# Two attention blocks on one core: query and key rows copied by transfers, masks as extra rows, neighbour products on GpSimd, attention values in one full-precision product

## What is computed

```python
# block 1 (_L1_conv_ref): attention over all 1024 positions
q = bn(q_w @ x); k = bn(k_w @ x)               # 16 rows each
v = bn(v_w @ x)                                # 128 rows
attn = softmax(einsum('bci,bcj->bij', q, k), axis=-1)
x = gamma * einsum('bcj,bij->bci', v, attn) + x
# block 2 (_L2_conv_ref)
af, sf = relu(bn(wa @ x)), relu(bn(ws @ x))    # 16 rows each
att = softmax(where(adj, af^T sf, NEG), axis=2)    # adj: the 8 neighbours of a pixel
h_s = einsum('bnm,bcm->bcn', att, x)
Gc = einsum('bcn,bdn->bcd', x, x)
catt = softmax(where(|c - d| == 1, Gc, NEG), axis=2)   # the two neighbour channels
x = (1 - gama) * x + gama * elu(h_s + catt @ x)
```

## Time and profile before

| | us |
|---|---|
| median of 3 runs | 290.1 (289.94 to 290.49) |
| the profiled execution | 290.33 |
| its span in the trace | 288.5 |
| PE busy | 272.3 |
| DVE busy | 213.2 |
| ACT busy | 186.2 |
| POOL busy | 95.1 |

### The profile page before, as it was taken

How to read it: one execution, slowest core, us unless ns; L and a number is a source line. 1 busy time by engine, 2 the same in 40 slices (tenths; PEclk the granted TensorE clock), 3 DMA queues, 4 the chain that set the end, 5 groups by cost and what they waited for, 6 DMA issues and landing times.

```text
span 288.5 us, 4440 instructions
## 1 busy us (share of the span) xinstructions
PE 272.3 (94%) x1499; PEld 178.6 (62%) x1499; DVE 213.2 (74%) x325; ACT 186.2 (65%) x355; POOL 95.1 (33%) x102
## 2 busy tenths in 40 slices
PE   7999999999999899999999999799999799999994
PEld 3846555467677576747657464467867557765462
DVE  3865889789998786763489867799788775828383
ACT  0774676789997474766648776688748457674320
POOL 1045031505236878128004101354279814000000
PEclk9999999999999999999999999979999999999998
DMA  6951000000000000000000000000000000000015
GB/s 184 353 202 51 0 1 1 2 0 1 3 0 1 0 2 0 1 3 0 0 3 1 0 2 1 1 0 2 1 0 2 1 0 3 2 4 0 2 73 220
DMA packets 4520, 8.14 MB, mean 28 GB/s; under 512 B 1118, under 2 KB 2014, under 8 KB 4498
## 3 DMA queue, kind: packets, MB, share of 16 engines
q1 hardware_dynamic: 4498, 7.85, 7.8%
HBM read 5.68 MB, written 2.10 MB: 27 GB/s over the span
## 4 chain that ended last, share of the span: by engine, by line
PE 66%; DVE 10%; POOL 8%; ACT 8%; issue 3%; DMA 2%; SPq 1%; DVEq 0%; POOLq 0%; ACTq 0%
PE psum L360 64%; POOL e1h L1047 4%; ACT e L686 3%; DVE e1l L900 3%; DMA qs<-row 2%; ACT psum L677 2%; POOL ks L1040 1%; DVE nmax L884 1%; POOL qs L1037 1%; SPq L348 1%; DVE nmax L850 1%; ACT qs L669 1%; POOL regionb L1010 1%; ACT ks L670 1%; DVE x L860 1%
## 5 line engine op out<-in xcount | busy, mean ns | idle before, releaser
L1047 POOL CAST e1h<-e 128x1024 fp32r<-128x1024 f32 x32 | 42.6, 1333 | 34.7 <-ACT e L686 21.6
L900 DVE TENSOR_TENSOR e1l<-e,e1h 128x1024 fp32r<-128x1024 f32 x32 | 40.8, 1282 | 9.8 <-POOL e1h L1047 9.7
L686 ACT ACTIVATE e<-psum 128x1024 f32<-128x1024 f32 x32 | 32.8, 1025 | 20.6 <-DVE e1l L900 15.7
L850 DVE TENSOR_REDUCE nmax<-psum 128x1 f32<-128x1024 f32 x32 | 39.0, 1221 | 9.3 <-PE psum L360 8.7
L657 ACT ACTIVATE e<-psum,nmax 128x1024 f32<-128x1024 f32 x32 | 35.7, 1115 | 14.2 <-issue 9.6
L884 DVE TENSOR_REDUCE nmax<-psum 128x1 f32<-128x1024 f32 x32 | 38.0, 1217 | 3.9 <-PE psum L360 3.8
L677 ACT ACTIVATE psum<-psum,nmax 128x1024 f32<-128x1024 f32 x32 | 34.8, 1089 | 7.0 <-DVE nmax L884 6.3
L360 PE MATMUL psum<-e,v0n 128*64 128x512 f32 x128 | 31.0, 604 | 0.0
L360 PE MATMUL psum<-ks,qs 96*128 96x512 f32 (+2 forms) x96 | 30.1, 405 | 0.8 <-DVE ks L874 0.4
L360 PE MATMUL psum<-qs,ks 96*128 96x512 f32 (+2 forms) x96 | 28.9, 389 | 1.8 <-DMA qs<-row 1.3
L360 PE MATMUL psum<-xh 128*128 128x512 f32 x64 | 28.3, 442 | 0.6 <-DVE x L860 0.3
(11 more groups left out here) (175 smaller groups left out, 491.4 us busy)
## 6 DMA issues: line engine op xcount, KB each, us to landing
out<-xin SPq DMA_DIRECT2D x8, 256.0 KB, 2.1
xin<-in_x SPq DMA_DIRECT2D x3, 512.0 KB, 6.1
twist<-in_twist_in SPq DMA_DIRECT2D x1, 768.0 KB, 7.4
zz<-in_region_in SPq DMA_DIRECT2D x2, 360.0 KB, 3.5
xin<-in_x SPq DMA_DIRECT2D x2, 256.0 KB, 2.8
untwist<-in_untwist_in SPq DMA_DIRECT2D x1, 512.0 KB, 7.2
zz<-in_near_in SPq DMA_DIRECT2D x1, 288.0 KB, 4.4
rw<-in_rows_w SPq DMA_DIRECT2D x1, 256.0 KB, 2.7
```

What stands on the lines that cost most here:

```text
L686: inc(go(e1[:, E1_AT[b, i], :], t[:, :], ACT.Exp), "e1_ready", b)
L850: inc(vec.tensor_reduce(nmax0[z][:, i:i + 1], t[:, :], AX.X, ALU.max, negate=True), "nmax0_ready", b)
L900: inc(vec.tensor_tensor(e1l[:, EH_AT[b, i], :], e1[:, E1_AT[b, i], :], e1h[:, EH_AT[b, i], :].bitcast(F32), ALU.subtract), "e1l_ready", b)
L1047: done(gp.tensor_copy(e1h[:, EH_AT[b, i], :], e1[:, E1_AT[b, i], :]), "e1h_ready", b, i)
```

## The change

- **q, k, a, s rows.** The projection repeats the 64 rows for both halves on 128 partitions. ACT writes the rounded 128x512 tile `hi` in one instruction, DVE the low part `lo` in one. SP copies them into `qs` and `ks` (now three groups of 17 rows, R = 17): eight transfers of 17 rows of 2048 bytes from `hi` (`qkhi`, `ashi`), four from `lo` (`qklo`, `aslo`). `score` and `near` wait for all twelve (`qk_in`, 192 counts). GpSimd's copies are gone, the bias of q and k is added by ACT and DVE.
- **Mask rows.** Once for each of the four tiles `qs` and `ks` (two each), SP copies 29 further rows of 4352 bytes (`nearin`), whose product with each other is hugely negative outside the neighbourhood. A near window is then one product; the mask product is gone.
- **Channel products.** Only the products of neighbour channels are formed: GpSimd multiplies `x2T` by itself shifted by a channel (`cprod`, 128x1016) and adds in three steps (`csum`, 508, 254 and 127 elements); PE has three float32 products of two, one and one columns. DVE spreads the two weights back to a matrix (three small instructions).
- **Values.** `attL`, `e1h`, `e1l` and the split of the values are gone: `attH` is one full float32 product for each half, two for each tile.
- Rings: `RING0` 5 to 7, `STAGE` 2 to 5. All order tables are new; SP has one of its own.

```diff
-RING0 = 5
-STAGE = 2
-RING = 3
+RING0 = 7
+STAGE = 5
+SP_STEPS = steps(
+    "qklo.0.0 regin.0.0 nearin.0.0 qkhi.0.0 row1.0.0 qkhi.1.0 qklo.1.0 row1.1.0 ashi.0.0 aslo.0.0 row2.0.0 "
...
+            def rows(dst, at, src, k, z):
+                for h in range(2):
+                    o = h * 2 * G + k * G
+                    sp.dma_start(dst[z][at * R:(at + 1) * R, W + h * HALF:W + (h + 1) * HALF].bitcast(F32),
+                                 src[z][o:o + R, :].bitcast(F32)).then_inc(s["qk_in"][z], 16)
...
+                elif name == "nearin":
+                    wait(sp, "nearr_ready", 0)
+                    for k in range(2):
+                        for n, dst in enumerate((qs, ks)):
+                            sp.dma_start(dst[k][KS3:KS4, :].bitcast(F32),
+                                         nearr[n * 32:n * 32 + MASKS, :].bitcast(F32)).then_inc(near_sem, 16)
...
+                elif name in ("qkhi", "ashi"):
+                    wait(sp, "hi_ready", b, int(name == "ashi"))
+                    for dst, at, k in ((qs, 0, 0), (ks, 0, 1), (qs, 1, 0), (ks, 2, 1)):
+                        rows(dst, at, hi, k, z)
+                elif name in ("qklo", "aslo"):
+                    wait(sp, "low_ready", b, int(name == "aslo"))
+                    for dst, at, k in ((qs, 2, 0), (ks, 1, 1)):
+                        rows(dst, at, lo, k, z)
...
                 elif name == "score":
-                    wait(pe, "dup_ready", b, 3)
-                    wait(pe, "low_ready", b, 1)
+                    pe.wait_ge(s["qk_in"][z], ROWS_IN * (b // 2 * 2 + 1))
...
                 elif name == "attH":
-                    wait(pe, "e1h_ready", b, i)
+                    wait(pe, "e1_ready", b, i)
...
-                    for k, vv in enumerate((v1h[z], v1l[z])):
-                        for h in range(2):
-                            ho = slice(h * HALF, (h + 1) * HALF)
-                            mm(t[:, ho], vv[:, i, :], e1h[:, EH_AT[b, i], ho], i == 0 and k == 0, False)
...
+                        last = mm(t[:, ho], v1[z][:, i, :], e1[:, E1_AT[b, i], ho], i == 0, i == CH - 1)
...
                 elif name == "chan":
-                    for u in range(CH):
-                        mm(t[:, 0:P], x2T[z][:, u, :], x2T[z][:, u, :], u == 0, False)
-                    end(step, mm(t[:, 0:P], identb[:], chainb[:], False, True))
+                    mm(t[:, 0:2], ident, edge[:], True, False, True)
+                    mm(t[:, 0:1], cgram[:, 0:P], one[:], False, False, True)
+                    end(step, mm(t[:, 1:2], cgram[:, 1:P + 1], one[:], False, True, True))
...
-                        mm(t[:, w0:w0 + WIN], identb[:], nearb[:, kind, :], first, False, True)
-                        last = mm(t[:, off:off + hi - lo], lhs[:, u * P:(u + 1) * P], rhs[:, lo:hi],
-                                  False, not first, True)
+                        last = mm(t[:, w0:w0 + WIN], lhs[:, W + u * P:W + (u + 1) * P], rhs[:, u * P:u * P + WIN],
+                                  True, True)
...
-                    inc(go(qs[z][0:G, hc], t[q, 0:HALF], func), "qhi_ready", b)
-                    inc(go(ks[z][2 * G:3 * G, hc], t[k, 0:HALF], func), "khi_ready", b)
+                        inc(go(hi[z][:], t[:, 0:HALF], ACT.Identity, bias=bias[:, QK:QK + 1]), "hi_ready", b)
```

More of the change, by code:

```diff
@@ L22 @@
 G = 32
-KS3 = 3 * G
+R = HID + 1
+KS3 = 3 * R
+MASKS = 29
+KS4 = KS3 + MASKS
 WIN = P + 2 * W
 WPAD = 256
+NW = N + 2 * W
+NEG = -2.0 ** 53
 M = 16
@@ L150 @@
     gram=lambda i: [("e0_ready", i)], mix=lambda i: [("x1_ready", 1)],
-    qkproj=lambda i: [("low_ready", 1)], asproj=lambda i: [("low_ready", 3)], val1=lambda i: [("v1_ready", 0)],
+    qkproj=lambda i: [("low_ready", 0)], asproj=lambda i: [("low_ready", 1)], val1=lambda i: [("v1_ready", 0)],
     score=lambda i: [("sum1_ready", i)], shift1=lambda i: [("row_ready", 0)], shift2=lambda i: [("row_ready", 1)],
@@ L216, in conv_seq @@
         xrow = sb("xrow", [P, 2 * P])
-        ident = sb("ident", [P, P])
-        chain = sb("chain", [P, P])
+        beside = sb("beside", [P, P + 2])
+        ident, above, below = beside[:, 1:P + 1], beside[:, 0:P], beside[:, 2:P + 2]
+        edge = sb("edge", [P, 2])
+        one = sb("one", [P, 1])
         turn = sb("turn", [P, 2 * P])
@@ L380, in _ @@
                     pe.wait_ge(s["wfold_ready"][0], 3)
-                    pe.wait_ge(s["ones_ready"][0], 1)
+                    pe.wait_ge(fill_ready, 1)
                     t = begin(step)
                     for k in range(3):
-                        last = nc.tensor.transpose(t[:, k * P:(k + 1) * P], rws[:, k, :], ident[:])
-                    for k in range(2):
-                        last = nc.tensor.transpose(t[0:3, (3 + k) * P:(4 + k) * P], bias3[:, k, :], ident[:])
-                    end(step, last)
+                        last = nc.tensor.transpose(t[:, k * P:(k + 1) * P], rws[:, k, :], ident)
+                    end(step, nc.tensor.transpose(t[0:3, 3 * P:4 * P], bias3[:], ident))
                 elif name == "gap":
@@ L596, in _ @@
                     t = begin(step)
-                    end(step, nc.tensor.transpose(t[:, 0:P], coef[z], ident[:]))
+                    end(step, nc.tensor.transpose(t[:, 0:P], coef[z], ident))
                 elif name == "i1":
@@ L663, in _ @@
                 elif name in ("qkproj", "asproj"):
-                    first, func = (0, ACT.Copy) if name == "qkproj" else (2, ACT.Relu)
-                    t = take((name, b, 0))
-                    if first:
-                        wait(act, "e1_ready", b, CH - 1)
-                    q, k = slice(2 * i * G, (2 * i + 1) * G), slice((2 * i + 1) * G, (2 * i + 2) * G)
-                    inc(go(qs[z][0:G, hc], t[q, 0:HALF], func), "qhi_ready", b)
-                    inc(go(ks[z][2 * G:3 * G, hc], t[k, 0:HALF], func), "khi_ready", b)
+                    t = take(step)
+                    if name == "qkproj":
+                        inc(go(hi[z][:], t[:, 0:HALF], ACT.Identity, bias=bias[:, QK:QK + 1]), "hi_ready", b)
+                    else:
+                        inc(go(hi[z][:], t[:, 0:HALF], ACT.Relu), "hi_ready", b)
                 elif name == "val1":
                     t = take(step)
-                    inc(go(v1h[z][:].rearrange("p u c -> p (u c)"), t[:, :], ACT.Copy), "v1h_ready", b)
+                    inc(go(v1[z][:].rearrange("p u c -> p (u c)"), t[:, :], ACT.Copy), "v1_ready", b)
                 elif name == "score":
@@ L862, in _ @@
                 elif name in ("qklow", "aslow"):
-                    first = 0 if name == "qklow" else 2
-                    t = take((name[:2] + "proj", b, 0))
-                    for hi, rows, ready, dst, to in ((qs[z], 2 * i, "qhi_ready", qs[z], 2), (ks[z], 2 * i + 1, "khi_ready", ks[z], 1)):
-                        exact = t[rows * G:(rows + 1) * G, 0:HALF]
-                        at = slice(0, G) if to == 2 else slice(2 * G, 3 * G)
-                        low = dst[to * G:(to + 1) * G, hc]
-                        wait(dve, ready, b, first + i)
-                        if first:
-                            last = vec.scalar_tensor_tensor(out=low, in0=exact, scalar=0.0, in1=hi[at, hc].bitcast(F32),
-                                                            op0=ALU.max, op1=ALU.subtract)
-                        else:
-                            last = vec.tensor_tensor(low, exact, hi[at, hc].bitcast(F32), ALU.subtract)
-                    inc(last, "low_ready", b)
-                elif name == "val1":
-                    t = take(step)
-                    wait(dve, "v1h_ready", b)
-                    inc(vec.tensor_tensor(v1l[z][:].rearrange("p u c -> p (u c)"), t[:, :],
-                                          v1h[z][:].rearrange("p u c -> p (u c)").bitcast(F32), ALU.subtract),
-                        "v1_ready", b)
+                    n = int(name == "aslow")
+                    t = take((name[0:2] + "proj", b, 0))
+                    wait(dve, "hi_ready", b, n)
+                    by, op = (0.0, ALU.max) if n else (bias[:, QK:QK + 1], ALU.add)
+                    inc(vec.scalar_tensor_tensor(out=lo[z][:], in0=t[:, 0:HALF], scalar=by, in1=hi[z][:].bitcast(F32),
+                                                 op0=op, op1=ALU.subtract), "low_ready", b)
                 elif name == "score":
@@ L1009, in _ @@
                     settle()
[L1010 removed]
+                    done(gp.tensor_copy(regionb[:, i], region), "regions_ready", 0, i)
                     if i == 1:
@@ L1133, in _pack @@
         rows_p[:, V, n] = i["L1_conv_v_" + part]
-    for g in range(2):
-        at = slice(g * G, g * G + HID)
+    for h, g in ((0, 0), (0, 1), (1, 0), (1, 1)):
+        at = slice((2 * h + g) * G, (2 * h + g) * G + HID)
         pre = "L1_conv_k_" if g else "L1_conv_q_"
```

250 lines of the change are left out of this document (132 added, 118 removed), and 150 rows, old and new, of tables (ACT_STEPS, DVE_STEPS, PE_TEXT, POOL_STEPS).

## The result

| | before | after |
|---|---|---|
| median of the runs, us | 290.3 (289.9 to 290.8, 4 runs) | 457.0 (455.2 to 458.3, 4 runs) |
| ratio to before, 95% interval | | 1.574 [1.568, 1.580] |
| span of the profiled execution | 288.5 | 453.5 |
| PE busy / idle | 272.3 / 16.2 | 301.4 / 152.1 |
| PE busy at half clock, as recorded | 3.4 | 61.6 |

The account below looks back on a forecast made before the run. PE's work plus its waits was taken to bound the kernel (PE busy 272.3 of 288.5 us). Work and vanishing waits -5.8, transfer waits +140.7 and clock +13.6 on 290.3 gave 438.8, said as 438; range 302 to 475 for 8 in 10.

Parts of the forecast that it names:

- One engine for 17 and 29 rows, about 24 GB/s: Row and mask transfers: a prime row count runs on one DMA engine, 1.45 us per 17-row transfer, 5.26 per mask transfer.
- The waits: PE between projection and score: first wait 37.0 us, seven others 103.7 in sum, +140.7 us in all.
- Covers: PE's work between a projection and its score, which hides part of the transfers: 4.0 to 7.6 us for the seven.
- Waits that go, -2.9: PE's waits of 1.5 and 1.4 us for GpSimd's copies vanish; bounds 0 and -9 for lighter engines giving PE more.
- The clock, +13.6: Half clock behind eight long PE waits, 1.7 us lost each; bounds 0 and 27.
- PE's work, -2.9: PE's own work: values +10.4, near windows -7.0, channel product -5, bias products -1.3 us.
- near windows: Mask and score product of 0.22 us become one of 0.11, 64 times: -7.0 us, bounds nothing and 8.5 gained.
- channel product: PE's mask and eight products of 1.92 us become three small ones of 0.7, four times: -5 us.
- values: 64 full float32 products of 0.86 us replace 192 one-pass matmuls of 0.2325 on PE: +10.4 us.
- bias products: Four pairs of bias products leave PE: -1.3 us, between -0.9 and -1.9.
- Channel products on GpSimd, latency: GpSimd's product and sums on the way to `chan`: bounds 0 to 18 us, taken at 0.
- The sum: Profiled execution 290.3 - 5.8 + 140.7 + 13.6 = 438.8 us; 438 was said.

Follow-up runs that it names:

- e1: Changed kernel with 18 rows for 17 in each q and k row transfer, 29-row mask transfers kept; 378.3 us, ratio 1.302.
- e2: Changed kernel with 19 rows for 17 in each row transfer; 470.4 us, ratio 1.619.
- e3: Changed kernel with 32 rows in each row transfer and 32 mask rows for 29, the added rows zeros; 337.2 us, ratio 1.161.
- e11: Kernel before with mask rows, full-precision values and channel products on GpSimd, all but the row transfers; 299.1 us, ratio 1.030.
- e12: Kernel before with mask rows and full-precision values, without channel products on GpSimd; 288.8 us, ratio 0.995.
- e5: Kernel before with the channel products on GpSimd alone, their steps moved as in the change; 304.9 us, ratio 1.050.
- e7: Kernel before with mask rows and channel products on GpSimd, engine copies and split values kept; 299.9 us, ratio 1.035.
- e6: Kernel before with the mask rows alone, q and k still copied by GpSimd; 286.9 us, ratio 0.988.

## Why the prediction was right, and which terms were off

- **One engine for 17 and 29 rows, about 24 GB/s.** Right, shown by the records, by the flat 23 to 27 GB/s, and by e1, e2 and e3. It carries most of the result: from e3 to the changed kernel 119.8 of 166.7 us. In the profiled executions this is 100.1 of idle time, 6.5 of clock and 10.3 of PE's work; the last has nothing to do with the DMA engine.
- **The waits.** 36.1 and 103.6 us for 37.0 and 103.7. The single ones differ by up to 0.8, both ways: 13.9, 16.7, 16.2, 11.8, 15.6, 13.9 and 15.5 for 14.1, 16.1, 16.2, 12.6, 14.9, 14.5 and 15.3. Covers taken from the trace of before were good enough; that the sum agrees to 0.1 is chance.
- **Waits that go, -2.9.** PE's idle time grew by 135.9 where the forecast had 140.7 - 2.9 = 137.8. The two new waits (1.8 and 2.4) are in the 135.9; without them and the long ones 8.2 us are left of the old 16.2. So -8.0 stands where I took -2.9, within the bound of -9.
- **The clock, +13.6: the term that was mis-sized.** It is 28.2, just beyond the upper bound of 27. I had taken one stretch of 3.4 us behind each wait, from one short gap. Behind the eight long waits PE worked 3.8 to 12.0 us at half clock, 24.1 us lost where 13.6 were forecast, and two stretches more stand at the start (6.8) and behind the wait for `xin` (6.6), which weren't in the list. The view of windows of one gap told that the clock falls, not how long it stays down.
- **PE's work, -2.9: measured +0.9.** Its parts were near: near windows -5.0 (-7.0), channel product -4.7 (-5), values +6.0 to +7.8 (+10.4), bias products -1.3 (-1.3). From e11 to e3 the work falls by 6.6: besides the bias products the new tables have seven filling products fewer (21 for 28, some 0.2 us each), and the score products take 3.3 us less from start to start, for which I have no reason. What no step of the forecast had is the +10.3 from e3 to the changed kernel, with the same steps in the same order. It lies beside the score products' 51 rows, below. That the sum comes out near the forecast is luck: two terms that it lacked nearly cancel.
- **Channel products on GpSimd, latency "taken at 0, since PE waits for the longer transfers anyway".** The condition was true for the changed kernel: neither `chan` nor `ecn` stands among PE's waits there. Without the long transfers the price is 10.3 us (e11 against e12), inside the 0 to 18 named. My expectations of e5, e7 and e11 forgot that condition, and missed.
- **The sum.** 438.8 against 455.2 of the profiled execution: clock +14.6, work +3.8, idle -1.9, in all 16.5.

Step by step, by medians: 290.3 before; mask rows -3.4; values +1.9; channel products +10.3; row transfers as such, 32 rows wide, +38.1; 17 rows for 32, +119.8. Only the first of these steps wins time. e6 is the fastest kernel of all, and e12 is the only other one below the kernel before. The steps were taken in this order alone; in another order their shares could differ.

## What to carry to other kernels

Count the rows of a transfer before its bytes: 17, 19 and 29 rows, primes above 16, each went over one DMA engine, and padding to 32 was cheaper than the rows saved. When a step moves to another engine, price its whole way back to PE with the covers of the kernel in which it will stand, and look which two-input operations of VectorE run beside GpSimd's. Every new wait of some microseconds on PE has a second price behind it, the work at half clock; count waits, not only their length.

## What the runs showed of the hardware beyond that

**Products over 51 rows beside products over 128 rows cost PE 0.4 us a round more than products over 96 rows do.** A round of one value step and two score tiles, in order of time, in the changed kernel (51 rows) and in e3 (96 rows), both at full clock:

```profile
139.12 1.98 PE L382 MATMUL psum<-e,v 128*128 128x512 f32 x4
141.04 0.73 PE L382 MATMUL psum<-ks,qs 51*128 51x512 f32 x2
141.61 0.63 PE L382 MATMUL psum<-qs,ks 51*128 51x512 f32 x2
142.16 1.98 PE L382 MATMUL psum<-e,v 128*128 128x512 f32 x4
```

```profile
100.59 1.88 PE L383 MATMUL psum<-e,v 128*128 128x512 f32 x4
101.91 1.03 PE L383 MATMUL psum<-ks,qs 96*128 96x512 f32 x2
102.78 0.62 PE L383 MATMUL psum<-qs,ks 96*128 96x512 f32 x2
103.23 1.88 PE L383 MATMUL psum<-e,v 128*128 128x512 f32 x4
```

3.04 us with 51 rows, 2.64 with 96: fewer rows are slower. The 2.64 are just two products of 0.86 and two tiles of 0.46. The same tables with 54 rows (e1) and with 57 (e2) give 3.04 us again, so it is the number of rows that decides, somewhere between 57 and 96. A round with three score tiles costs 0.4 us more as well (3.49 for 3.12), so the price goes with the change between the two kinds of product, not with the number of tiles. The Trainium skill (TensorEngine Tiling (Array Packing), Key Properties) says that a change of the tiling mode drains TensorE, and the list of modes on the same page has one of 64 rows beside that of 128. 51, 54 and 57 rows would fit the first, 96 only the second. The rounds agree with this, but the trace shows no mode, so the effect of the rows is measured and the reason is argued.

**The price of an issue from SP**, start to start, was 0.60 to 0.64 us for one engine (17 rows, each of 2 KB), 0.74 for nine (18 rows) and 0.63 for sixteen (32 rows); why nine cost most no run shows. With one-engine transfers an issue takes 1.1 to 1.7 us once several are queued, and up to 5 behind the mask rows.

**The clock's price hardly depends on a wait's length**: from 20 us on, behind the start, 27.1 us went to it with eight waits of 62 us in all (e1), 27.4 with 140 (the changed kernel), 26.2 with 156 (e2) and 20.5 with 39 (e3).
